# A sampling-and-scan loop: factors from three row groups, three selection banks, long matmuls set apart, GpSimd's sums in a row

## The chip, the cores and the metric

The kernel runs on one core of one Trainium2 chip. The metric is device time in microseconds (us) of one execution; the kernel before took 2436.45 us (median of three runs, 2435.26 to 2442.39).

## The reference, cut to what matters

Four convolutional blocks follow each other on a batch of 4 images of 64 channels and 128x128 pixels. Only the third block's second half matters here. Its input has been through a depthwise convolution; offsets were computed from it, and then:

```
out = tap(y0,x0,(1-wy)(1-wx)) + tap(y0,x0+1,(1-wy)wx) + tap(y0+1,x0,wy(1-wx)) + tap(y0+1,x0+1,wy*wx)   # bilinear sampling
x_dbl = x_proj_w @ out            # 8 rows for dt, 1 row B, 1 row C
delta = softplus(dt_w @ x_dbl[:8] + dt_b);   dA = exp(delta * A);   dBx = delta * B * out
h[t] = dA[t] * h[t-1] + dBx[t];   y[t] = C[t] * h[t] + Ds * out[t]    # along all pixels
x = x + out_proj( layernorm(y) )
```

## The kernel before, in words

Two images stand on the 128 partitions at once (2 x 64 channels), so the whole program runs twice ("pairs"). In the sampling loop an image pair is cut into 32 tiles of 4 rows, 128 x 512 elements. The offsets are small, so sampling is done with nine shifts: each pixel's nine factors are computed in a compact form (`W9`), split into three bf16 parts, transposed by a DMA into `WTB`, spread over the channels by TensorE, multiplied with the shifted image on VectorE, and the nine products are summed (four on TensorE into the bank `ACC`, five on GpSimd).

The loop is a software pipeline written out by hand. Each engine runs `step` for c = -2 to 35; `on(d)` says whether tile c+d exists, and the order of the statements in `step` is the order in the engine's queue, which is strict. T is the tile of step c. Semaphores count steps, `after(t)` is the count once tile t is done. All names below are used in the text that follows:

- VectorE (`sample_and_scan_dve`): `product(q)`, q = 0 to 8 (L856) reads the factors that `spread(q)` put in a PSUM bank; `t` (L863) and `x` (L867) scale and add the block's output for tile T-4; `bx` (L875), `scan` (L881), `hc` (L892) and `y` (L897) are the recurrence for tile T-2; `delta` (L907) is the softplus' last sum for tile T-1. `y` waits for `proj` of tile T-3, since it overwrites `YY`.
- TensorE (`sample_and_scan_pe`): `spread(q)` (L1066, bf16) alternates between two PSUM banks and waits for product q-2; `add_up(m)` (L1074, f32) sums product m; `center` (L1082), `mean` (L1090) and `proj` (L1092) are the layernorm and output projection of tile T-3; `WZ`, `WB`, `WC` (L1105, L1111, L1115) make the factors z, B and C of tile T-1 directly from the sampled tile with three f32 matmuls. In front of `WZ` the queue waits for GpSimd's last sum of tile T-1, for `delta` and for `scan` of tile T-2 (`sc_h`).
- ScalarE (`sample_and_scan_act`): hat functions of the offsets (L1004, L1008), `hi`, `mid` copies (L1041, L1043), square, Ln and Exp of the layernorm (L999, L1020, L1022), softplus of z (L1025 to L1030), the copy of the sampled tile out of `ACC` (L1035), and dA (L1048).
- GpSimd (`sample_and_scan_pool`): the factors (L955, L964, L970), the five sums `add(m)` (L948) and `UU` = delta times the sampled tile (L977).
- SyncE issues the DMA transposes, and at the kernel's start the loads of constants and the save `rt_spill`, whose landing (`rt_saved`) ScalarE and GpSimd wait for.

The lines that decide the order on TensorE around the three factor matmuls are, before:

```
                spread(5)
                if on(-1):
                    pe.wait_ge(df_add, summed(T - 1, POOL_SUMS - 1, POOL_SUMS))
                    pe.wait_ge(sc_delta, after(T - 2))
                    pe.wait_ge(sc_h, after(T - 2))
                    pe.matmul(PSUM[:, ZB, :], WZ[:, :], XS[:, (k + 1) % 2, :], ...).then_inc(sc_z, 1)
                spread(6)
```

Of the kernel before, what the change touches and what calls it, by code (L numbers as in the profile page):

```python
# [30 lines left out]
DT_RANK = 8  # L31
PW = W + 2
# [85 lines left out]
def program(nc, x, vec, mat, dts, rows, fc, sel, far_sel, cst, out):  # L118
    ctx = ExitStack()
    with ctx:  # L120
# [3 lines left out]
        def sem(name):  # L124
# [11 lines left out]
        WQ, WK, WV, WPROJ, WIN, WZ, WB, WC = (sb(n, [P, P]) for n in  # L136
            ("WQ", "WK", "WV", "WPROJ", "WIN", "WZ", "WB", "WC"))
# [30 lines left out]
        DTS = REG[0:DT_RANK, NMAT + 62 * P:NMAT + 62 * P + 3 * C]  # L168
# [110 lines left out]
        assert NMAT + 62 * P + 3 * C <= NREG - TOK - NRT  # L279
# [34 lines left out]
        ACC, ZB, BB, CB, MB, OB2 = 2, 3, 4, 5, 6, 7  # L314
# [15 lines left out]
        def steps(*ns):  # L330
# [37 lines left out]
        (sc_z, sc_bc, sc_abs, sc_exp, sc_ln, sc_delta, sc_u, sc_da, sc_bx, sc_h, sc_hc, sc_y, sc_cen, sc_proj, sc_sq, sc_var,  # L368
         sc_lv, sc_rs, sc_t, sc_x) = (sem(n) for n in (
            "sc_z", "sc_bc", "sc_abs", "sc_exp", "sc_ln", "sc_delta", "sc_u", "sc_da", "sc_bx", "sc_h", "sc_hc",  # L370
            "sc_y", "sc_cen", "sc_proj", "sc_sq", "sc_var", "sc_lv", "sc_rs", "sc_t", "sc_x"))
# [70 lines left out]

        def strip_done(pair, c):

            return pair * NS + (c + 1)
# [40 lines left out]
        def _(sp):  # L486
# [4 lines left out]
            sp.dma_start(DTS[:, :], dts).then_inc(load, 16)  # L491
# [12 lines left out]
            sp.wait_ge(const_act, 3)  # L504
            sp.dma_start(rt_spill, RT).then_inc(rt_saved, 16)
# [3 lines left out]
            with sp.Fori(0, PAIRS) as pair:  # L509
# [76 lines left out]
                sp.wait_ge(sc_delta, pair * NT + (NT + CREDIT))  # L586
# [244 lines left out]
        def sample_and_scan_dve(dve, pair, stats):  # L831
# [3 lines left out]
            def step(pair, c, b, on, far=False):  # L835
                T, k = pair * NT + c, b % 2

                def product(q):
                    if not on(0):
                        return  # L840
                    dy, dx = TAPS[q]
                    dve.wait_ge(df_w, turn(T, q))

                    if q == 0:
                        dve.wait_ge(df_acc, summed(T - 1, 3, PE_SUMS))
                    elif q == 1 and on(-1):
# [12 lines left out]
                product(0)
                if on(-4):  # L860
                    dve.wait_ge(sc_rs, after(T - 4))
                    dve.wait_ge(sc_proj, after(T - 4))
                    dve.tensor_tensor(PSUM[:, OB2, :], PSUM[:, OB2, :], RS2, ALU.mult).then_inc(sc_t, 1)  # L863
                product(1)
                if on(-4):
                    dve.wait_ge(sc_t, after(T - 4))
                    dve.scalar_tensor_tensor(out=xch(c - 4), in0=img(PSUM[:, OB2, :]), scalar=OUTB[:, :], in1=xch(c - 4),  # L867
                                             op0=ALU.add, op1=ALU.add,
                                             accum_out=sum_at[:, bass.ds(c - 4, 1)]).then_inc(sc_x, 1)
# [13 lines left out]
                if far and on(-1):  # L883

                    if on(0):
                        dve.wait_ge(df_acc, summed(T, PE_SUMS - 1, PE_SUMS))
                    dve.wait_ge(df_add, summed(T - 1, POOL_SUMS - 1, POOL_SUMS))
                    far_dve(dve, c - 1, (k + 1) % 2, reach)
                product(4)
# [12 lines left out]
                if on(-1):  # L902

                    dve.wait_ge(sc_ln, after(T - 1))
                    dve.wait_ge(sc_u, after(T - 2))
                    dve.wait_ge(sc_da, after(T - 2))
                    dve.tensor_tensor(RL, PSUM[:, ZB, :], AB, ALU.add).then_inc(sc_delta, 1)  # L907
# [14 lines left out]
        def sample_and_scan_pool(pool, pair):  # L922
# [9 lines left out]
            def step(pair, c, b, on, far=False):  # L932
# [26 lines left out]
                add(0)  # L959
# [5 lines left out]
                add(1)  # L965
                if on(2):
# [11 lines left out]
                add(3)  # L978
# [3 lines left out]
        def sample_and_scan_act(act, pair):  # L982
# [7 lines left out]
            def step(pair, c, b, on, far=False):  # L990
# [5 lines left out]
                if on(-3):  # L996
                    act.wait_ge(sc_cen, after(T - 3))
                    act.wait_ge(sc_t, after(T - 4))
                    act.activation(RS2, PSUM[:, MB, :], ACT.Square).then_inc(sc_sq, 1)  # L999
                if on(2):  # L1000
# [7 lines left out]
                    act.activation(HT, HT, ACT.Relu, bias=1.0, scale=-1.0).then_inc(df_hat, 1)  # L1008
                if on(-4):
# [7 lines left out]
                if on(-3):  # L1017

                    act.wait_ge(sc_var, after(T - 3))
                    act.activation(RS2, PSUM[:, MB, :], ACT.Ln, bias=GNE[:, 1:2]).then_inc(sc_lv, 1)  # L1020
                    act.wait_ge(sc_lv, after(T - 3))
                    act.activation(RS2, RS2, ACT.Exp, scale=-0.5).then_inc(sc_rs, 1)  # L1022
                if on(-1):
                    act.wait_ge(sc_z, after(T - 1))
                    act.activation(AB, PSUM[:, ZB, :], ACT.Abs, bias=vc("dt_b")).then_inc(sc_abs, 1)  # L1025
                    act.wait_ge(sc_abs, after(T - 1))
                    act.activation(PSUM[:, ZB, :], PSUM[:, ZB, :], ACT.Relu, bias=vc("dt_b"))
                    act.activation(AB, AB, ACT.Exp, scale=-1.0).then_inc(sc_exp, 1)
                    act.wait_ge(sc_exp, after(T - 1))
                    act.activation(AB, AB, ACT.Ln, bias=1.0).then_inc(sc_ln, 1)  # L1030
# [5 lines left out]
                if on(2):  # L1036
# [5 lines left out]
                    act.wait_ge(df_r1, after(T + 2))  # L1042
                    act.activation(part(1), top(REST), ACT.Copy).then_inc(df_mid, 1)  # L1043
                if on(-1):

                    act.wait_ge(sc_delta, after(T - 1))
                    act.wait_ge(sc_h, after(T - 2))
                    act.activation(DA, RL, ACT.Exp, scale=SM[:, 9:10]).then_inc(sc_da, 1)  # L1048
# [3 lines left out]
        def sample_and_scan_pe(pe, pair):  # L1052
# [3 lines left out]
            def step(pair, c, b, on, far=False):  # L1056
                T, k = pair * NT + c, b % 2

                def spread(q):

                    if on(0):
# [3 lines left out]
                        pe.wait_ge(df_p, turn(T, q - 2))  # L1065
                        pe.matmul(img(PSUM[:, (k + q) % 2, :]), SELB[:, q, :], WTB[0:WROWS, k, :, h, :],  # L1066
# [12 lines left out]
                if on(-3):  # L1079
                    pe.wait_ge(sc_y, after(T - 3))  # L1080
                    pe.wait_ge(sc_lv, after(T - 4))
                    pe.matmul(PSUM[:, MB, :], cs("center"), YY, start=True, stop=True).then_inc(sc_cen, 1)  # L1082
# [3 lines left out]
                add_up(1)  # L1086
                spread(4)
                if on(-3):
                    pe.wait_ge(sc_sq, after(T - 3))
                    pe.matmul(PSUM[:, MB, :], cs("mean"), RS2, start=True, stop=True).then_inc(sc_var, 1)  # L1090
                    pe.wait_ge(sc_x, after(T - 4))
                    pe.matmul(PSUM[:, OB2, :], WOUT2[:, :], YY, start=True, stop=True).then_inc(sc_proj, 1)  # L1092
                add_up(2)
                spread(5)
                if far:
                    add_up(3)
                if on(-1):
# [7 lines left out]
                    pe.matmul(PSUM[:, ZB, :], WZ[:, :], XS[:, (k + 1) % 2, :], start=True, stop=True).then_inc(sc_z, 1)  # L1105
                spread(6)
                if not far:
                    add_up(3)
                spread(7)
                if on(-1):  # L1110
                    pe.matmul(PSUM[:, BB, :], WB[:, :], XS[:, (k + 1) % 2, :], start=True, stop=True)  # L1111
                spread(8)
                if on(-1):
                    pe.wait_ge(sc_y, after(T - 2))
                    pe.matmul(PSUM[:, CB, :], WC[:, :], XS[:, (k + 1) % 2, :], start=True, stop=True).then_inc(sc_bc, 1)  # L1115
# [53 lines left out]
        def _(dve):  # L1169
# [4 lines left out]
            dve.wait_ge(load, 16 * 9)  # L1174

            for w in (WQ, WK, WV, WPROJ, WIN, WOUT, WZ, WB, WC):
                dve.memset(w[:, :], 0.0)
# [27 lines left out]
            for s in range(2):  # L1205
# [5 lines left out]
                xp = MAT["x_proj"][0]  # L1211
                for w, col in ((WB, DT_RANK), (WC, DT_RANK + 1)):
                    dve.tensor_copy(w[p:q, p:q], MATS[p:q, xp + col:xp + col + 1].broadcast_to([C, C]))
# [37 lines left out]
            for s in range(2):  # L1251
                p, q = s * C, s * C + C
                dve.tensor_copy(WZ[p:q, p:q], PSUM[p:q, 0, 0:C])
# [1231 lines left out]
```

## Time and profile before

| | |
|---|---|
| median of three runs | 2436.45 us |
| the profiled execution's own time | 2439.82 us |
| its span in the trace | 2438.0 us |
| busy share of the span: PE, DVE, ACT, POOL | 88%, 75%, 58%, 58% |
| granted TensorE clock, mean over the span | 0.929 |
| the two sampling loops | about 743 to 1110 us and 1938 to 2305 us |

In the trace PE is TensorE's matmul and PEld its weight load, DVE is VectorE, ACT ScalarE, POOL GpSimd and SP SyncE; L856 is line 856 of the kernel before. The span is what the trace covers; the execution's own time is 1.8 us longer. A record's duration overlaps the next one's on the same engine (VectorE's 128x512 operations last some 0.68 us and start 0.60 us apart), so distances between starts are what a queue costs. An f32 matmul of 512 columns shows as two records.

### The profile page before, as it was taken

What the parts mean: (1) busy time and instruction counts of PE and PEld (TensorE: products, weight loads), DVE (VectorE), ACT (ScalarE), POOL (GpSimd) and SP (SyncE); (2) the same over time, 40 slices, a digit from 0 to 9 for tenths busy, and PEclk for the clock granted to TensorE, in tenths of its full rate; (3) what the DMA queues carried; (4) which work ended last, traced back from release to release, by engine and by line L of the source; (5) the groups of instructions that cost most, each with busy time, mean ns of one, the idle gap of its engine ahead of it and who ended that gap; (6) DMA issues with size and microseconds to landing.
All of it is one profiled execution on the core that took longest, in us unless ns stands there. A gap on an engine that the chain in (4) does not pass through costs nothing. (4 is left out here: it accounts for less than half of the span.)

```text
span 2438.0 us, 28756 instructions
## 1 busy us (share of the span) xinstructions
PE 2135.2 (88%) x7363; PEld 1102.2 (45%) x7363; DVE 1834.2 (75%) x3128; ACT 1416.5 (58%) x2192; POOL 1417.2 (58%) x1305
## 2 busy tenths in 40 slices
PE   2998759798998999997988978698989799999798
PEld 2397435443553444433335954353435434444243
DVE  6555667499986999995755658566999589999754
ACT  1843444286884777763346437235868667777532
POOL 2233009398967989972322410484989499999532
PEclk9978879899998999998998979799989799999899
DMA  5000283500001212224820006534000022223244
GB/s 189 1 1 0 92 302 94 199 1 1 1 1 28 44 39 61 40 52 141 251 45 0 1 1 233 189 107 158 0 1 1 12 27 53 48 44 61 83 122 113
DMA packets 199339, 172.78 MB, mean 71 GB/s; under 512 B 72535, under 2 KB 175327, under 8 KB 195831
## 3 DMA queue, kind: packets, MB, share of 16 engines
q1 hardware_dynamic: 199159, 170.78, 24.8%
q8 instruction: 64, 1.05, 0.2%
q14 instruction: 116, 0.95, 0.1%
HBM read 81.69 MB, written 72.29 MB: 63 GB/s over the span
## 5 line engine op out<-in xcount | busy, mean ns | idle before, releaser
L948 POOL TENSOR_TENSOR BIG<-BIG 128x512 f32<-128x512 f32 x320 | 407.1, 1272 | 88.4 <-DVE BIG L856 78.4
L856 DVE TENSOR_TENSOR BIG<-PSUM,BIG 128x512 f32<-128x512 f32 x576 | 391.0, 682 | 59.0 <-PE PSUM L1066 30.7
L1138 DVE SCALAR_TENSOR_TENSOR PSUM<-BIG,VECS,PSUM 128x1024 f32<-128x1024 f32 x224 | 288.2, 1287 | 44.6 <-PE PSUM L2111 39.5
L1074 PE MATMUL PSUM<-BIG,CSTS 128*128 128x512 f32 x512 | 266.8, 602 | 0.0
L782 POOL TENSOR_TENSOR BIG<-TOEP,BIG 128x384 f32<-128x384 f32 x84 | 98.2, 1196 | 270.5 <-DVEq L1543 270.5
L2111 PE MATMUL PSUM<-BIG,WDW 128*128 128x512 f32 x512 | 236.4, 607 | 11.1 <-ACT BIG L2011 11.1
L1066 PE MATMUL PSUM<-BIG,SELB 120*128 120x512 bf16 x576 | 212.0, 386 | 16.7 <-issue 6.8
L2307 PE MATMUL PSUM<-BIG 128*128 128x381 f32 (+1 forms) x576 | 189.5, 493 | 12.9 <-DVE BIG L789 12.9
L1066 PEld LDWEIGHTS PSUM<-BIG,SELB 120*128 120x128 bf16 x576 | 55.3, 96 | 264.4 <-DVE BIG L856 190.9
L2111 PEld LDWEIGHTS PSUM<-BIG,WDW 128*128 128x128 f32 x512 | 99.3, 195 | 141.1 <-issue 122.4
L1784 POOL TENSOR_TENSOR BIG<-BIG 128x1024 f32<-128x1024 f32 x64 | 151.1, 2360 | 10.3 <-POOL BIG L1787 10.3
L2307 PEld LDWEIGHTS PSUM<-BIG 128*128 128x128 f32 x576 | 111.4, 194 | 90.5 <-ACT BIG L1962 13.5
L741 PE MATMUL PSUM<-BIG,WL 128*128 128x512 f32 x256 | 120.9, 617 | 15.2 <-POOL BIG L726 12.3
L725 POOL TENSOR_TENSOR BIG<-BIG 128x576 f32<-128x576 f32 x32 | 38.8, 1214 | 152.9 <-issue 92.6
L1074 PEld LDWEIGHTS PSUM<-BIG,CSTS 128*128 128x128 f32 x512 | 98.2, 195 | 58.6 <-issue 54.2
L1787 POOL TENSOR_SCALAR BIG<-BIG,VECS,CSTS 128x1024 f32<-128x1024 f32 x96 | 114.3, 1197 | 17.1 <-DVE PSUM L1593 11.2
L741 PE MATMUL PSUM<-BIG,WMID 128*128 128x512 f32 x256 | 115.3, 593 | 0.2 <-DVE BIG L716 0.2
L1972 ACT ACTIVATE BIG<-PSUM,SMG 128x1152 f32<-128x1152 f32 x32 | 39.1, 1221 | 121.7 <-PE PSUM L2307 108.4
L1793 POOL TENSOR_TENSOR BIG<-BIG 128x1024 f32<-128x1024 f32 x32 | 75.6, 2362 | 55.5 <-ACT BIG L1999 55.1
L1025 ACT ACTIVATE BIG<-PSUM,VECS 128x512 f32<-128x512 f32 x64 | 44.0, 687 | 108.4 <-PE PSUM L1105 108.4
L1999 ACT ACTIVATE BIG<-BIG,VECS 128x1024 f32<-128x1024 f32 x96 | 102.9, 1139 | 0.0
L1549 DVE SCALAR_TENSOR_TENSOR BIG<-BIG,SMG 128x1152 f32<-128x1152 f32 x32 | 54.2, 1693 | 54.6 <-ACT BIG L1972 54.6
(363 smaller groups left out, 5079.6 us busy)
## 6 DMA issues: line engine op xcount, KB each, us to landing
spill<-X SPq DMA_DIRECT2D x18, 1024.0 KB, 6.1
back_spill<-BIG SPq DMA_DIRECT2D x32, 576.0 KB, 3.4
X<-x SPq DMA_DIRECT2D x32, 512.0 KB, 7.5
rows_spill<-X SPq DMA_DIRECT2D x64, 256.0 KB, 4.1
out<-BIG SPq DMA_DIRECT2D x64, 256.0 KB, 3.6
BIG<-rows_spill SPq DMA_DIRECT2D x28, 512.0 KB, 5.3
X<-back_spill SPq DMA_DIRECT2D x14, 896.0 KB, 12.8
BIG<-fc SPq DMA_DIRECT2D x8, 1024.0 KB, 10.0
```

Source lines behind the costliest of these rows:

```text
L741: ins = pe.matmul(PSUM[:, 4 * k + m, :].rearrange("p (r j) -> p r j", r=8), w, VC[:, k, m, b:b + 8, :], start=(b == 0), stop=(b == 1))
L782: eng.tensor_tensor(to.rearrange("p (x c r) -> p x c r", x=3, r=WROW), TOEP[:, y].unsqueeze(1).unsqueeze(1).broadcast_to([P, 3, WCH, WROW] ...
L856: dve.tensor_tensor(img(product_buffer(b, q)), img(PSUM[:, (k + q) % 2, :]), pch(c, XBASE, dy, dx), ALU.mult).then_inc(df_p, 1)
L948: pool.tensor_tensor(a, a, x, ALU.add).then_inc(df_add, 1)
L1066: pe.matmul(img(PSUM[:, (k + q) % 2, :]), SELB[:, q, :], WTB[0:WROWS, k, :, h, :], start=True, stop=True).then_inc(df_w, 1)
L1074: pe.matmul(PSUM[:, ACC, :], ident, product_buffer(b, m), start=(m == 0), stop=(m == PE_SUMS - 1)).then_inc(df_acc, 1)
L1138: return dve.scalar_tensor_tensor(out=rows8(to), in0=strip(c, base, dy, dx), scalar=vc(weights, j), in1=rows8(acc), op0=ALU.mult, op1=ALU.add)
L1784: pool.tensor_tensor(d_side[:, c % 2, :], d_side[:, c % 2, :], d_tap, ALU.add).then_inc(d1_part, 1)
L1787: pool.tensor_scalar(rows8(d_tap if n else d_side[:, c % 2, :]), strip(c, XBASE, dy, dx), vc("dw_w", DW2_SIDE[n]), cs("zero")[:, 0:1], ALU ...
L1999: act.activation(rows8(a_side[:, j, c % 2, :]), strip(c, BASE, dy, dx), ACT.Identity, scale=vc("conv2d_w", j)).then_inc(d1_side, 1)
L2111: ins = pe.matmul(img(acc[:, h * CH:(h + 1) * CH]), w[:, j - stored, :], strip(c, base, dy, dx)[:, h * ROWS:(h + 1) * ROWS, :], start=(j = ...
L2307: ins = pe.matmul(to, WIDE[:, u % RING, x, :], v, start=(x == 1), stop=(x == 2))
```

## The change

On TensorE the three factor matmuls are replaced by two stages: `WX` (one f32 matmul of the sampled tile onto 96 rows: three groups of 32 rows, each with the ten rows of `x_proj` for both images), a copy of these 96 rows by ScalarE into `AB`, and then three f32 matmuls with 32 contracted rows each (`WG`), one per group, that write z, B and C into their banks. `spread` rotates over three banks (0, 1, 7) and waits for product q-3; `proj` writes the bank `MB`, which `center` and `mean` use too, so it now waits for Ln (`sc_lv`). The f32 matmuls are set apart by spreads. VectorE's `delta` moves from the end of step T-1's tile to the middle of the next step, `bx`, `scan` and `hc` follow each other behind product 4. GpSimd does its split first and then `add(0)` to `add(3)` without other work between. On ScalarE the `mid` copy and dA move to the next step's beginning, and the copy for `WX` is added. The buffers of the products are assigned differently. At the start the load of `dts` and the product that made `WZ` go, and six small loads of `WG` are issued ahead of `rt_spill`.

```diff
-        ACC, ZB, BB, CB, MB, OB2 = 2, 3, 4, 5, 6, 7
+        ACC, ZB, BB, CB, MB = 2, 3, 4, 5, 6
+        SPREADS = (0, 1, 7)
...
             sp.wait_ge(const_act, 3)
+            for s in range(2):
+                at, cols = s * XR, slice(s * C, (s + 1) * C)
+                sp.dma_start(WG[at:at + DT_RANK, cols], dts[:, 2 * C:3 * C]).then_inc(load, 16)
+                for r in (1, 2):
+                    row = r * 32 + at + DT_RANK + r - 1
+                    sp.dma_start(WG[row:row + 1, cols], cst[0:1, CST["one"][0]:CST["one"][0] + C]).then_inc(load, 16)
             sp.dma_start(rt_spill, RT).then_inc(rt_saved, 16)
...
# VectorE, step
                product(1)
                if on(-4):
...
+                if on(-2):
+                    dve.wait_ge(sc_ln, after(T - 2))
+                    dve.wait_ge(sc_u, after(T - 3))
+                    dve.wait_ge(sc_da, after(T - 3))
+                    dve.tensor_tensor(RL, PSUM[:, ZB, :], AB, ALU.add).then_inc(sc_delta, 1)
                 product(2)
+                product(3)
+                if not far:
+                    product(4)
                 if on(-2):
                     dve.wait_ge(sc_u, after(T - 2))
-                    dve.wait_ge(sc_bc, after(T - 2))
+                    dve.wait_ge(sc_zbc, all_three(T - 2))
                     dve.tensor_tensor(PSUM[:, BB, :], UU, PSUM[:, BB, :], ALU.mult).then_inc(sc_bx, 1)
-                product(3)
-                if on(-2):
                     dve.wait_ge(sc_bx, after(T - 2))
...
-                product(4)
                 if on(-2):
                     dve.wait_ge(sc_h, after(T - 2))
                     dve.tensor_tensor(PSUM[:, CB, :], HH[:, k, :], PSUM[:, CB, :], ALU.mult).then_inc(sc_hc, 1)
...
                 product(8)
-                if on(-1):
-                    dve.wait_ge(sc_ln, after(T - 1))
...
# GpSimd, step (after the three multiplies of W9)
-                add(0)
...
-                add(1)
...
+                add(0)
+                add(1)
                 add(2)
+                add(3)
                 if on(-1):
                     pool.wait_ge(sc_delta, after(T - 1))
...
-                add(3)
                 add(4)
# ScalarE, step
+                if on(-1):
+                    act.wait_ge(sc_xd, after(T - 1))
+                    act.wait_ge(sc_delta, after(T - 2))
+                    act.activation(AB[0:3 * 32, :], PSUM[0:3 * 32, ZB, :], ACT.Copy).then_inc(sc_copied, 1)
# TensorE, step
-                        pe.wait_ge(df_p, turn(T, q - 2))
-                        pe.matmul(img(PSUM[:, (k + q) % 2, :]), SELB[:, q, :], WTB[0:WROWS, k, :, h, :],
+                        if q >= 3 or on(-1):
+                            pe.wait_ge(df_p, turn(T, q - 3))
+                        pe.matmul(img(PSUM[:, SPREADS[q % 3], :]), SELB[:, q, :], WTB[0:WROWS, k, :, h, :],
                                   start=True, stop=True).then_inc(df_w, 1)
```

TensorE's order in one step is then, with its waits (those between `spread(6)` and `WX` are the old ones in front of `WZ`, unchanged):

```
spread 0, 1, 2; add_up 0; spread 3; add_up 1; center; spread 4; add_up 2; spread 5; mean; spread 6;
[wait df_add(T-1), sc_delta(T-2), sc_h(T-2)] WX; spread 7; [wait sc_lv(T-3)] proj; add_up 3; spread 8;
[wait sc_copied(T-1), sc_y(T-2)] three row-group matmuls
```

VectorE's is: product 0, t, product 1, x, delta, products 2, 3, 4, bx, scan, hc, product 5, [wait sc_proj(T-3)] y, products 6, 7, 8.

## Rows read from the trace of the kernel before

**Rows 1.** Windows: stretch, length, then busy us of PE, PEld, DVE, ACT, POOL; clock; DMA.
```profile
900.00:1000.00 100.00, 99.82 (x269) 41.11 (x268) 96.12 (x158) 74.04 (x156) 90.22 (x101) 1.00 0.22 45
```
**Rows 2.** Timeline of VectorE, one step: start us, duration us, line, operation, [idle before].
```profile
904.18 0.68 DVE L856 TENSOR_TENSOR BIG<-PSUM,BIG 128x512 f32<-128x512 f32 x1
...
905.98 0.74 DVE L867 SCALAR_TENSOR_TENSOR X<-PSUM,OUTB,X 128x512 f32<-128x512 f32 x1
...
906.64 0.69 DVE L856 TENSOR_TENSOR BIG<-PSUM,BIG 128x512 f32<-128x512 f32 x1
...
908.44 1.27 DVE L881 TENSOR_TENSOR_SCAN BIG<-BIG,PSUM 128x512 f32<-128x512 f32 x1
...
913.84 0.69 DVE L856 TENSOR_TENSOR BIG<-PSUM,BIG 128x512 f32<-128x512 f32 x1 [0.21 <-PE PSUM L1066]
...
917.51 0.68 DVE L856 TENSOR_TENSOR BIG<-PSUM,BIG 128x512 f32<-128x512 f32 x1
...
919.31 1.27 DVE L881 TENSOR_TENSOR_SCAN BIG<-BIG,PSUM 128x512 f32<-128x512 f32 x1
```
**Rows 3.** Timeline of TensorE, the same step.
```profile
907.39 0.39 PE L1066 MATMUL PSUM<-BIG,SELB 120*128 120x512 bf16 x1
907.61 1.02 PE L1090 MATMUL PSUM<-BIG,CSTS 128*128 128x512 f32 x2
908.48 1.02 PE L1092 MATMUL PSUM<-BIG,WOUT 128*128 128x512 f32 x2
...
913.43 0.38 PE L1066 MATMUL PSUM<-BIG,SELB 120*128 120x512 bf16 x1
```
**Rows 4.** Timeline of VectorE: the stage's first scan, then its end.
```profile
767.62 1.27 DVE L881 TENSOR_TENSOR_SCAN BIG<-BIG,SM,PSUM 128x512 f32<-128x512 f32 x1
...
1082.30 1.27 DVE L881 TENSOR_TENSOR_SCAN BIG<-BIG,PSUM 128x512 f32<-128x512 f32 x1
...
1090.81 0.70 DVE L875 TENSOR_TENSOR PSUM<-BIG,PSUM 128x512 f32<-128x512 f32 x1 [0.41 <-POOL BIG L977]
1091.54 1.28 DVE L881 TENSOR_TENSOR_SCAN BIG<-BIG,PSUM 128x512 f32<-128x512 f32 x1
1092.85 0.70 DVE L892 TENSOR_TENSOR PSUM<-BIG,PSUM 128x512 f32<-128x512 f32 x1
...
1097.23 0.69 DVE L907 TENSOR_TENSOR BIG<-PSUM,BIG 128x512 f32<-128x512 f32 x1 [2.90 <-ACT BIG L1030]
...
1109.88 0.75 DVE L867 SCALAR_TENSOR_TENSOR X<-PSUM,OUTB,X 128x512 f32<-128x512 f32 x1
```
**Rows 5.** Timeline at the stage's end: a TensorE matmul behind a wait, then ScalarE.
```profile
1093.45 1.12 PE L1105 MATMUL PSUM<-BIG,WZ 128*128 128x512 f32 x2 [1.13 <-POOL BIG L948]
1094.42 1.02 PE L1111 MATMUL PSUM<-BIG,WB 128*128 128x512 f32 x2
1094.62 0.69 ACT L1025 ACTIVATE BIG<-PSUM,VECS 128x512 f32<-128x512 f32 x1 [1.76 <-PE PSUM L1105]
```
**Rows 6.** Timeline of TensorE in the attention: row-group matmuls between full ones.
```profile
1441.07 1.13 PE L2197 MATMUL PSUM<-BIG 32*128 32x256 f32 x8
1442.14 1.09 PE L2210 MATMUL PSUM<-CSTS,BIG 128*128 128x128 f32 x8
1443.16 1.13 PE L2197 MATMUL PSUM<-BIG 32*128 32x256 f32 x8
```
**Rows 7.** Timeline at the kernel's start: SyncE's issues, and ScalarE that waits for them.
```profile
49.77 0.33 SPq L505 DMA_DIRECT2D rt_spill<-BIG  x1
50.14 0.48 SPq L507 DMA_DIRECT2D rows_spill<-CSTS  x1
...
52.69 0.60 SPq L508 DMA_DIRECT2D rows_spill<-CSTS  x1
...
54.81 1.28 ACT L1858 ACT_TABLE_LOAD   x1 [5.07 <-DMA rows_spill<-CSTS]
56.63 0.26 ACT L1852 ACTIVATE SM<-PSUM,GNE 128x1 f32<-128x1 f32 x1 [0.54 <-PE PSUM L2105]
```

More of the change, by code:

```diff
@@ L882, in step @@
                                            ALU.mult, ALU.add).then_inc(sc_h, 1)
[L883 to L888, printed above, removed]
-                product(4)
+                if far:
+                    if on(-1):
+                        if on(0):
+                            dve.wait_ge(df_acc, summed(T, PE_SUMS - 1, PE_SUMS))
+                        dve.wait_ge(df_add, summed(T - 1, POOL_SUMS - 1, POOL_SUMS))
+                        far_dve(dve, c - 1, (k + 1) % 2, reach)
+                    product(4)
                 if on(-2):
@@ L995, in step @@
                     act.preload_act_table_set("natural_log_exp_and_others")
[L996 to L999, printed above, removed]
+                if on(1):
+                    act.wait_ge(df_r1, after(T + 1))
+                    act.activation(part(1), top(REST), ACT.Copy).then_inc(df_mid, 1)
                 if on(2):
@@ L1016, in step @@
                                    bias=SHIFT, accum_out=sq_at[:, c - 4:c - 3]).then_inc(stats_done, 1)
[L1017 to L1022, printed above, removed]
-                if on(-1):
[L1024 to L1030, printed above, removed]
+                if on(-1):
+                    act.wait_ge(sc_xd, after(T - 1))
+                    act.wait_ge(sc_delta, after(T - 2))
+                    act.activation(AB[0:3 * 32, :], PSUM[0:3 * 32, ZB, :], ACT.Copy).then_inc(sc_copied, 1)
                 if on(0):
@@ L1078, in step @@
                 spread(1)
[L1079 to L1082, printed above, removed]
                 spread(2)
@@ L1086, in step @@
                 add_up(1)
+                if on(-3):
+                    pe.wait_ge(sc_y, after(T - 3))
+                    pe.wait_ge(sc_x, after(T - 4))
+                    pe.matmul(PSUM[:, MB, :], cs("center"), YY, start=True, stop=True).then_inc(sc_cen, 1)
                 spread(4)
+                add_up(2)
+                spread(5)
                 if on(-3):
@@ L1090, in step @@
                     pe.matmul(PSUM[:, MB, :], cs("mean"), RS2, start=True, stop=True).then_inc(sc_var, 1)
[L1091 to L1094, printed above, removed]
+                spread(6)
                 if far:
@@ L1104, in step @@
                         far_pe(pe, c - 1, reach)
[L1105 to L1106 removed]
+                    pe.matmul(PSUM[:, ZB, :], WX[:, :], XS[:, (k + 1) % 2, :], start=True, stop=True).then_inc(sc_xd, 1)
+                spread(7)
+                if on(-3):
+                    pe.wait_ge(sc_lv, after(T - 3))
+                    pe.matmul(PSUM[:, MB, :], WOUT2[:, :], YY, start=True, stop=True).then_inc(sc_proj, 1)
                 if not far:
                     add_up(3)
[L1109 to L1111 removed]
                 spread(8)
                 if on(-1):
+                    pe.wait_ge(sc_copied, copied(T - 1, 0))
                     pe.wait_ge(sc_y, after(T - 2))
[L1115 removed]
+                    settle(pe)
+                    for r, bank in enumerate((ZB, BB, CB)):
+                        rows = slice(r * 32, r * 32 + 32)
+                        pe.matmul(PSUM[:, bank, :], WG[rows, :], AB[rows, :], start=True, stop=True).then_inc(sc_zbc, 1)
             settle(pe)
@@ L1173, in _ @@
             dve.reg_mov(far_dve_turn, 0)
[L1174 to L1176 removed]
+            dve.wait_ge(load, 16 * 8)
+            for w in (WQ, WK, WV, WPROJ, WIN, WOUT, WX, WG):
                 dve.memset(w[:, :], 0.0)
```

92 lines of the change are left out of this document (48 added, 44 removed).

## The prediction

> **What bounds the kernel now.** The windows come first: in the steady sampling loop PE is busy 99.8 of 100 us, DVE 96.1, POOL 90.2 and ACT 74.0, at the full TensorE clock, 2.4 GHz [rows 1]. So three engines stand close together, and shares do not tell which one sets the step. The timeline does: scans follow each other by 10.87 us (908.44 to 919.31 [rows 2]), and one circle of waits adds up to just that. Product 8 starts at 913.84, product 2 of the next step 3.67 us later, behind VectorE's own work; 0.75 us after a product 2 (906.64) comes spread 4 (907.39), which waits for it because there are two banks; from there TensorE runs to spread 8 without a gap, 6.04 us (907.39 to 913.43), and 0.41 us later product 8 starts [rows 2, 3]. 3.67 + 0.75 + 6.04 + 0.41 = 10.87. The reader should see that the step is neither VectorE's nor TensorE's sum, but a chain that changes engines twice.
>
> **Prices.** VectorE's tensor-tensor operations start 0.60 us apart (904.18 to 905.98 holds three), the scalar-tensor-tensor ones 0.66 (905.98 to 906.64) [rows 2]. One that waits for the operation directly in front of it costs more: bx to scan 0.73, scan to hc 1.31 [rows 4]. A spread takes 0.22, an f32 matmul 0.87, its record 1.02 [rows 3]; behind a wait an f32 matmul takes 0.97 to the next one [rows 5]. A reader of PSUM starts 0.03 to 0.05 us after the record's end (913.43 + 0.38 to 913.84; 1093.45 + 1.12 to 1094.62) [rows 2, 3, 5]; I take 0.05 for TensorE behind VectorE too.
>
> **Part 1, the banks and the long matmuls.** With three banks spread q waits for product q-3, and the circle above is gone. What is left on VectorE is the sum of its queue: nine products 5.40, t, delta and hc 1.80, x and y 1.32, bx 0.73, scan 1.31, together 10.56 us; bx, scan and hc now stand in a row and pay 0.25 of it. TensorE's sum is nine spreads 1.98, eight f32 matmuls 6.96 (four add_ups, center, mean, proj, WX), the three row groups and the change to them and back.
>
> **Part 2, the row groups.** The loop before has none; the attention has. There eight records of 32 contracted rows and 256 columns and eight full ones of 128 columns take 2.09 us together (1441.07 to 1443.16) [rows 6]. From 0.87 for two passes of 512 columns, a pass of 256 is 0.217 and one of 128 is 0.109. One after another the first eight alone would take 1.74 and all 2.61; in pairs they take 0.87, with the eight full ones 1.74, and 0.35 is left for going over and back. So row groups do run side by side, and I price the three at 0.87 + 0.35. The lower bound is 0.87; the upper, one after another, 2.61 + 0.35. TensorE's sum: 1.98 + 6.96 + 1.22 = 10.16 us.
>
> The Trainium skill (TensorE: Matmul & The Clock Gate, Part 3: Packing small matmuls) gives four row groups of 512 columns a speed-up of 3.07 instead of 4. By that page three groups would take an estimated 4 x 0.87 / 3.07 = 1.13 instead of 0.87, and the time would come out some 14 us above mine; rows 6 show full overlap, but of two groups only.
>
> **Part 3, what takes the old circle's place.** The wait in front of WX is the one that stood in front of WZ: scan of tile T-2 must be done. Before, scan came behind product 3 and TensorE met the wait late. Now scan stands behind delta and product 4, and spread 7, proj, add_up 3, spread 8 and the row groups are all queued behind WX. VectorE's y waits for proj, because YY is overwritten. That closes a circle:
> - scan to y: scan 1.27, start 0.05, WX 0.97, spread 7 0.22, proj 1.02, start 0.03: 3.56 us (VectorE alone would reach y after 1.31 + 0.60 + 0.60 = 2.51).
> - y to the next scan, VectorE's queue without a gap: y 0.66, products 6 to 8 1.80, product 0, t, product 1 1.80, x 0.66, delta 0.60, products 2 to 4 1.80, bx 0.73: 8.05 us.
>
> Together 11.61. A second circle goes through spread 0 of the next step, which stands behind the row groups: scan 1.27, 0.05, WX 0.97, spread 7 0.22, proj 0.87, add_up 0.87, spread 8 0.22, row groups 0.87, over and back 0.35, spread 0 to product 0 0.39 + 0.03: 6.11; product 0 to scan 1.80 + 0.66 + 0.60 + 1.80 + 0.73 = 5.59: 11.70. A third goes through the softplus: to the row groups' end 5.75, Abs to delta 2.61 (1094.62 to 1097.23 [rows 4, 5]), delta to scan 3.13: 11.49. The longest sets the step: **11.70 us, 0.83 more than before**. Is TensorE at WX by the time scan ends? In that order it has passed spread 6 about 0.4 us after scan starts, so yes: it then idles about 0.9 us.
>
> The Trainium skill (VectorE: DVE Perf Modes, The DRAIN you can't avoid) says that a semaphore between chained operations costs nothing extra. By that page bx to scan would be 0.60, each circle 0.13 shorter, and the time an estimated 7 us below mine; rows 4 show 0.73, so the trace disagrees.
>
> **What is hidden.** ScalarE gets one more copy, at most the 0.69 of an Abs [rows 5]: 7.4 + 0.7 = 8.1 us a step, with room; the copy itself lies beside spread 7, proj, add_up and spread 8 (2.18 us), and longer than that it would delay the row groups one for one. GpSimd's 9.0 us a step [rows 1] are only reordered; its UU waits for the later delta, and bx for UU: from delta's start 0.7 + 1.3 against 2.4 us of products, so 0.4 is spare. The mid copy and with it the DMA transpose move to the next step's start; spread 0 that reads the result comes some 8 us after, and if that cover went, product 0 would wait. The six small loads are needed only hundreds of us later.
>
> **Sum.** Between the first scan and the one at 1082.30 lie 29 steps, 314.68 us, 10.85 each [rows 4]. After: 27 at 11.70, and two at some 11.0, in which t, x and proj are still missing: 337.9, so +23.2 us. The fill before the first scan has the third bank and no scan to wait for: -1 (-2.5 to +1). The end, from 1082.30 to the last x at 1109.88, is a chain of single operations [rows 4]: the last tile's factors now need a copy and the groups (0.7 + 0.35 + 0.87 = +1.9), WX waits for the scan before it (+1.2), and proj for Ln (about +1): +4 (1 to 7). That is 26.2 for a pair, 52.4 for two. At the start SyncE issues six small loads ahead of rt_spill, at 0.37 (49.77 to 50.14) to 0.73 us each (49.77 to 52.69 holds four): 2.2 to 4.4; ScalarE's table load waits for the end of these issues and has 0.54 spare [rows 7]; VectorE's and SyncE's shorter preparation gives up to 1 back: +2 (0 to 4). In all +54. The sum is made on the profiled execution, whose own 2439.82 us (span 2438.0) are 3.4 above the median; I put the difference on the median, 2436.45: **2490 us**.
>
> **Rivals.**
> - *Faster:* WX's wait is already met when TensorE comes to it (as it would be if it asked for the scan of a tile earlier), and VectorE's sum is the step: 10.56, or -0.31 for 54 steps, -17, and +8 from the fill, the ends and the start: 2428 us. It decides if TensorE passes spread 6 later than scan ends, 0.9 us from my reckoning, and even then scan to y stays a chain. For it: the third bank removes today's circle. Against: the order in the code.
> - *The groups do not run side by side*, so that factors by groups save nothing: circle two gets 1.74 longer, 13.4 a step, 54 times: 2584 us. Against: rows 6.
> - *The clock falls.* PE idles about 1.5 of 11.7 us; if it were granted 1.2 GHz, circle one's WX, spread and proj would double, +2.2 a step: 2609 us; half the time, 2550. For it: idle gaps that rows 1 do not have; against: they are short.
>
> **How the numbers follow.** My forecast gets 0.80, the faster rival 0.10, the groups 0.05, the clock 0.05. The forecast's own bounds: circles of 11.4 to 12.0 us (54 times -0.3 to +0.3, 16 us), the fill, ends and start -12 to +13 (their ranges above, added up but for a third): 2462 to 2519; I let the upper end reach to 2525, towards a clock that falls in some steps. That leaves out the rivals, 2 in 10. A measurement tells 0.3%, 7 us, from no change. The faster rival lies just beyond that bound, so it is split: faster 0.07, same 0.03, slower 0.90.
>
> **What would show it.** Scans 11.7 us apart; PE idle in front of WX, released by scan; y with an idle time released by proj, or product 0 by spread 0; the three groups within a few hundredths of a us of each other, followed by the next spread after about 1.1; PE busy near 87%. Wrong if scans are under 10.9 us apart, if VectorE shows no idle at y and at product 0, or if the clock in the loop is below 1.0.

## The result, and the profile after

The changed kernel takes 2510.56 us (median of four runs, 2507.08 to 2513.3); the kernel before 2439.15 (four runs, the three from ahead of the prediction among them). The ratio is 1.0293, 95% interval 1.0269 to 1.0316: 71 us slower, where +54 and 2490 us were forecast. The profiled execution's span is 2511.5 us, against 2438.0 before, +73.5.

The windows of the changed kernel, over the same stretch and with the same columns as [rows 1]:

```profile
900.00:1000.00 100.00, 91.39 (x265) 32.87 (x263) 89.05 (x143) 73.25 (x151) 84.65 (x96) 1.00 0.21 43
```

Every engine is less busy than before, and the clock is still at its full level, 2.4 GHz. So no engine's sum sets the step; something is waited for. The page's costliest groups name it (busy us, mean ns; idle us before, and what ended most of it):

```profile
L1122 PE MATMUL PSUM<-BIG,WX 128*128 128x512 f32 x128 | 73.1, 653 | 49.8 <-DVE BIG L897 48.2
```

L897 is the scan, L1122 is WX: TensorE stands 48 us in front of WX until a scan is done, 0.75 for each of 64 tiles. Two timelines show what that does. VectorE, one step (start, duration, line, operation, [idle before, what ended it]), to be read beside [rows 2]; L897 is scan, L914 y, L865 the products, L893 bx:

```profile
911.98 1.28 DVE L897 TENSOR_TENSOR_SCAN BIG<-BIG,PSUM 128x512 f32<-128x512 f32 x1
...
915.69 0.75 DVE L914 SCALAR_TENSOR_TENSOR BIG<-BIG,VECS,PSUM 128x512 f32<-128x512 f32 x1 [1.11 <-PE PSUM L1126]
916.35 2.48 DVE L865 TENSOR_TENSOR BIG<-PSUM,BIG 128x512 f32<-128x512 f32 x4
...
923.01 0.69 DVE L893 TENSOR_TENSOR PSUM<-BIG,PSUM 128x512 f32<-128x512 f32 x1
923.73 1.28 DVE L897 TENSOR_TENSOR_SCAN BIG<-BIG,PSUM 128x512 f32<-128x512 f32 x1
```

TensorE, the same step; L1084 is spread, L1126 proj, L1137 the row groups:

```profile
912.31 0.38 PE L1084 MATMUL PSUM<-BIG,SELB 120*128 120x512 bf16 x1
913.41 1.10 PE L1122 MATMUL PSUM<-BIG,WX 128*128 128x512 f32 x2 [0.71 <-DVE BIG L897]
914.34 0.38 PE L1084 MATMUL PSUM<-BIG,SELB 120*128 120x512 bf16 x1
914.56 1.02 PE L1126 MATMUL PSUM<-BIG,WOUT 128*128 128x512 f32 x2
...
916.28 0.38 PE L1084 MATMUL PSUM<-BIG,SELB 120*128 120x512 bf16 x1
916.59 1.13 PE L1137 MATMUL PSUM<-BIG,WG 32*128 32x512 f32 x6
917.65 1.03 PE L1084 MATMUL PSUM<-BIG,SELB 120*128 120x512 bf16 x3
```

Scans are 11.75 us apart. The circle reads off the two fences: scan 911.98, WX 913.41, proj 914.56, y 915.69 after 1.11 us of idle, and from y VectorE works without a gap to the next scan, 8.04 us. 3.71 + 8.04 = 11.75. Product 0 of the next step, the last of the four products at 916.35, has no gap in front of it, so the circle through spread 0 is not the one that binds: spread 0's record ends at 918.03 (917.65 + 0.38), product 0 starts at 918.15 (the fourth of the four, 3 x 0.60 behind 916.35), some 0.1 us later than it had to.

**Where the 73.5 us lie.** On VectorE, first scan, last scan of the steady steps, the y that waits, and the last t and x of the first pair, to be read beside [rows 4]:

```profile
769.02 1.28 DVE L897 TENSOR_TENSOR_SCAN BIG<-BIG,SM,PSUM 128x512 f32<-128x512 f32 x1
...
1112.05 1.28 DVE L897 TENSOR_TENSOR_SCAN BIG<-BIG,PSUM 128x512 f32<-128x512 f32 x1
...
1128.52 0.75 DVE L914 SCALAR_TENSOR_TENSOR BIG<-BIG,VECS,PSUM 128x512 f32<-128x512 f32 x1 [3.18 <-PE PSUM L1126]
...
1148.12 0.70 DVE L872 TENSOR_TENSOR PSUM<-PSUM,BIG 128x512 f32<-128x512 f32 x1 [7.92 <-PE PSUM L1126]
1148.86 0.75 DVE L876 SCALAR_TENSOR_TENSOR X<-PSUM,OUTB,X 128x512 f32<-128x512 f32 x1
```

| stretch | before | after | difference | forecast |
|---|---|---|---|---|
| pair 1: start to the first product 0 | 743.96 | 745.37 | +1.4 | +2 |
| first product 0 to first scan | 23.66 | 23.65 | 0.0 | -1 |
| 29 steady steps | 314.68 | 343.03 | +28.4 | +23.2 |
| the end, from the last steady scan to the last x | 27.58 | 36.81 | +9.2 | +4 |
| between the pairs' loops | 828.74 | 829.86 | +1.1 | 0 |
| pair 2: the same three stretches | 365.90 | 399.24 | +33.3 | +26.2 |
| the rest | 133.48 | 133.54 | +0.1 | 0 |

Pair 2's are -0.6, +25.0 (339.64 against 314.65) and +8.9 (36.51 against 27.58). The steps carry 53 us of the loss, where 46 were forecast; the two ends carry 18, where 8 were.

TensorE at the end of the first pair (L1104 is center, L1110 mean) shows why:

```profile
1119.85 1.10 PE L1104 MATMUL PSUM<-BIG,CSTS 128*128 128x512 f32 x2 [2.06 <-DVE X L876]
1121.63 2.07 PE L1110 MATMUL PSUM<-BIG,CSTS 128*128 128x512 f32 x2 [0.69 <-ACT BIG L1022]
1124.75 2.05 PE L1122 MATMUL PSUM<-BIG,WX 128*128 128x512 f32 x2 [1.05 <-DVE BIG L897]
...
1140.36 2.05 PE L1104 MATMUL PSUM<-BIG,CSTS 128*128 128x512 f32 x2 [2.67 <-DVE X L876]
1143.09 2.08 PE L1110 MATMUL PSUM<-BIG,CSTS 128*128 128x512 f32 x2 [0.69 <-ACT BIG L1022]
1145.94 2.08 PE L1126 MATMUL PSUM<-BIG,WOUT 128*128 128x512 f32 x2 [0.78 <-ACT BIG L1031]
```

Two things are to be seen. An f32 matmul that takes 1.02 to 1.13 us elsewhere takes 2.05 to 2.08 here: the clock is at its lower level, 1.2 GHz, again and again. And center waits for VectorE's x of the tile before, proj for ScalarE's Ln, because center, mean, proj, t and x all use the bank MB and take turns. The same fall of the clock stands at the loop's beginning, where TensorE idles 2.36 us until the first scan is done:

```profile
770.45 2.04 PE L1122 MATMUL PSUM<-BIG,WX 128*128 128x512 f32 x2 [2.36 <-DVE BIG L897]
...
772.71 1.92 PE L1092 MATMUL PSUM<-BIG,CSTS 128*128 128x512 f32 x2
```

The first interval between scans is 13.74 us there. In pair 2 TensorE idles the same 2.36 us at that place, the clock does not fall, and the interval is 10.74.

### The profile page after: what moved, and what is told of

Same layout as the page of the kernel before. It is cut to its first block and busy times, and to the rows that moved or that the text cites. A ratio compares the mean times of both kernels' runs of the same rounds, so it can differ in the third digit from the quotient of the medians.

```text
span 2511.5 us, 29190 instructions
## 1 busy us (share of the span) xinstructions
PE 2135.8 (85%) x7489; PEld 1065.2 (42%) x7489; DVE 1838.0 (73%) x3123; ACT 1458.3 (58%) x2256; POOL 1425.8 (57%) x1305
## 5 line engine op out<-in xcount | busy, mean ns | idle before, releaser
L865 DVE TENSOR_TENSOR BIG<-PSUM,BIG 128x512 f32<-128x512 f32 x576 | 367.2, 683 | 33.9 <-PE PSUM L1084 24.9
L1092 PE MATMUL PSUM<-BIG,CSTS 128*128 128x512 f32 x512 | 277.8, 624 | 15.2 <-DVE BIG L865 15.0
L796 POOL TENSOR_TENSOR BIG<-TOEP,BIG 128x384 f32<-128x384 f32 x84 | 83.6, 1023 | 272.4 <-DVEq L1561 272.4
L1084 PE MATMUL PSUM<-BIG,SELB 120*128 120x512 bf16 x576 | 209.8, 386 | 12.0 <-DMA BIG<-BIG 7.8
L1092 PEld LDWEIGHTS PSUM<-BIG,CSTS 128*128 128x128 f32 x512 | 87.0, 190 | 126.7 <-DVE BIG L865 95.5
L1084 PEld LDWEIGHTS PSUM<-BIG,SELB 120*128 120x128 bf16 x576 | 52.4, 97 | 185.6 <-issue 126.5
L1122 PE MATMUL PSUM<-BIG,WX 128*128 128x512 f32 x128 | 73.1, 653 | 49.8 <-DVE BIG L897 48.2
L1051 ACT ACTIVATE BIG<-PSUM 128x512 f32<-128x512 f32 x64 | 38.3, 598 | 107.8 <-PE PSUM L1092 106.0
```

The source lines that it names most:

```text
L865: dve.tensor_tensor(img(product_buffer(b, q)), img(PSUM[:, SPREADS[q % 3], :]), pch(c, XBASE, dy, dx), ALU.mult).then_inc(df_p, 1)
L1084: pe.matmul(img(PSUM[:, SPREADS[q % 3], :]), SELB[:, q, :], WTB[0:WROWS, k, :, h, :], start=True, stop=True).then_inc(df_w, 1)
L1092: pe.matmul(PSUM[:, ACC, :], ident, product_buffer(b, m), start=(m == 0), stop=(m == PE_SUMS - 1)).then_inc(df_acc, 1)
L1122: pe.matmul(PSUM[:, ZB, :], WX[:, :], XS[:, (k + 1) % 2, :], start=True, stop=True).then_inc(sc_xd, 1)
```

## The experiments

Theory: the wait for scan in front of WX closes a circle, scan, WX, proj, y, scan, and that circle is the step. Rivals: another circle of the same length stands right behind it (through spread 0, or the softplus), so that the wait alone is worth little; or VectorE's new order (bx, scan and hc in a row) costs the time. The first four runs share one set of times of the kernel before (median 2434.71 us), the last four another (2434.58).

**no_scan_wait.** WX no longer waits for scan; the waits for delta of tile T-2 (in front of WX) and for y of tile T-2 (in front of the row groups) stay, and these cover the banks that are overwritten. (The branch `far`, for larger offsets, keeps the wait.)

```diff
                     pe.wait_ge(df_add, summed(T - 1, POOL_SUMS - 1, POOL_SUMS))
                     pe.wait_ge(sc_delta, after(T - 2))
-                    pe.wait_ge(sc_h, after(T - 2))
```

> The changed kernel without the wait for scan in front of WX (its results are still safe: the row groups, which overwrite the banks that scan reads, wait for y, and y follows scan). Theory: the circle scan - WX - spread 7 - proj - y - next scan sets the step. Then WX starts when spread 6 is through, 0.55 us behind scan's start instead of 1.43, proj starts behind it at about 1.6 (Ln is done at 1.2), y comes 2.7 behind scan instead of 3.7 and the step falls from 11.75 to 10.7 to 10.9 us: about 2450 to 2460 us. Rival 1: y waits for proj because proj now shares its bank and waits for Ln; then WX moves but y does not: 11.7 a step, about 2510. Rival 2: the row groups' own circle (through spread 0 and the softplus) is as long as it was reckoned with the scan wait: 11.4 to 11.6 a step, about 2490 to 2500.

Measured: 2448.04 us, ratio 1.0060 (1.0038 to 1.0081). TensorE, then VectorE:

```profile
957.67 1.02 PE L1122 MATMUL PSUM<-BIG,WX 128*128 128x512 f32 x2
...
958.75 1.02 PE L1126 MATMUL PSUM<-BIG,WOUT 128*128 128x512 f32 x2
```
```profile
957.11 1.28 DVE L897 TENSOR_TENSOR_SCAN BIG<-BIG,PSUM 128x512 f32<-128x512 f32 x1
...
959.88 0.75 DVE L914 SCALAR_TENSOR_TENSOR BIG<-BIG,VECS,PSUM 128x512 f32<-128x512 f32 x1 [0.16 <-PE PSUM L1126]
960.54 2.48 DVE L865 TENSOR_TENSOR BIG<-PSUM,BIG 128x512 f32<-128x512 f32 x4
...
967.91 1.28 DVE L897 TENSOR_TENSOR_SCAN BIG<-BIG,PSUM 128x512 f32<-128x512 f32 x1
```

WX starts 0.56 us after scan starts, without idle; y's gap shrinks from 1.11 to 0.16 and the step is 10.80. This one wait, an old line that the change left alone, holds all the loss in the steps: without it they are 0.07 us shorter than before. Yet the kernel is still slower than the one before, because its ends (35.05 us from the last steady scan to the last x) are 7.5 us longer than [rows 4] shows, in each pair.

**proj_first.** The wait stays, proj is moved ahead of it. This was meant to open the circle through y and to leave the one through spread 0.

```diff
                 spread(6)
+                [wait sc_lv(T-3)] proj
                 [wait df_add(T-1), sc_delta(T-2), sc_h(T-2)] WX
                 spread(7)
-                [wait sc_lv(T-3)] proj
                 add_up(3)
```

> The changed kernel with the scan wait kept, but proj stands ahead of WX in TensorE's queue. Theory: two circles of nearly the same length; the one through y is opened (proj ends 2.4 behind scan's start, before y is due at 2.5), the one through WX, add_up, the row groups and spread 0 stays: product 0 about 6.0 behind scan, 11.6 a step, about 2500 us; VectorE's idle time moves from y to products 8 and 0. Rival: the stall at y is all there is; then it goes and the step is 10.7 to 10.8, about 2455.

Measured: 2490.94 us, ratio 1.0234 (1.0196 to 1.0272), step 11.57. VectorE's scan, y and, behind products 6 to 8, product 0; then TensorE's proj, WX, spreads 0 to 2 and add_up 0 (L1092):

```profile
950.77 1.28 DVE L897 TENSOR_TENSOR_SCAN BIG<-BIG,PSUM 128x512 f32<-128x512 f32 x1
...
953.29 0.74 DVE L914 SCALAR_TENSOR_TENSOR BIG<-BIG,VECS,PSUM 128x512 f32<-128x512 f32 x1
...
956.75 0.69 DVE L865 TENSOR_TENSOR BIG<-PSUM,BIG 128x512 f32<-128x512 f32 x1 [0.69 <-PE PSUM L1084]
```
```profile
952.04 1.12 PE L1114 MATMUL PSUM<-BIG,WOUT 128*128 128x512 f32 x2 [0.56 <-ACT BIG L1031]
953.01 1.02 PE L1125 MATMUL PSUM<-BIG,WX 128*128 128x512 f32 x2
...
956.32 0.82 PE L1084 MATMUL PSUM<-BIG,SELB 120*128 120x512 bf16 x3
957.49 1.12 PE L1092 MATMUL PSUM<-BIG,CSTS 128*128 128x512 f32 x2 [0.35 <-DVE BIG L865]
```

The idle time moved from y to product 0, released by a spread (L1084), and time and step came near what the theory expected. But the circle that binds here is another one. Scan is over at 952.05 and WX starts only at 953.01, straight behind proj: it is proj, now ahead of WX, that waits 0.56 us, for ScalarE's Ln (L1031). From product 0 the way goes to add_up 0 (0.74), over add_up 1, center and mean to Ln and proj (6.12, to 963.61), to WX (0.97), to the next spread 0 (3.31) and to product 0 (0.43), together 11.57, and scan is not on it. So the run put one wait in front of WX in the place of another; it does not show the circle through scan and spread 0. Moving proj gains 0.18 us a step, removing the wait for scan 0.95.

**products_between.** no_scan_wait with VectorE's order changed: products 5, 6 and 7 stand between bx, scan, hc and y, as products did in the kernel before.

```diff
-bx, scan, hc, product 5, y, products 6, 7, 8
+bx, product 5, scan, product 6, hc, product 7, y, product 8
```

> As no_scan_wait, and VectorE's order is product 4, bx, product 5, scan, product 6, hc, product 7, y, product 8, so that no operation waits for the one right in front of it. Rival (VectorE's queue is the bound once the scan wait is gone): its sum falls from 10.56 to 10.3 and the step by 0.2, 10 us below no_scan_wait. Theory of circles: y is now some 1.8 us later behind scan, and the row groups wait for y; from y's end over the groups (1.1) and spread 0 to product 0, and over the softplus to delta (3.9), the way is longer than VectorE's work beside it: 11.2 to 11.4 us a step, 2480 to 2490, slower than no_scan_wait though VectorE has less to do.

Measured: 2480.69 us, ratio 1.0182 (1.0141 to 1.0223), step 11.36. VectorE's y and product 0, then TensorE's row groups (L1140 here):

```profile
955.68 0.74 DVE L919 SCALAR_TENSOR_TENSOR BIG<-BIG,VECS,PSUM 128x512 f32<-128x512 f32 x1
...
958.02 0.69 DVE L865 TENSOR_TENSOR BIG<-PSUM,BIG 128x512 f32<-128x512 f32 x1 [1.00 <-PE PSUM L1087]
```
```profile
956.52 1.13 PE L1140 MATMUL PSUM<-BIG,WG 32*128 32x512 f32 x6 [0.55 <-issue]
957.59 0.82 PE L1087 MATMUL PSUM<-BIG,SELB 120*128 120x512 bf16 x3
```

VectorE's self-waits are gone, 0.25 us of its sum by the prediction's prices, and yet the step is 0.56 longer than in no_scan_wait: the row groups wait for y (955.68 + 0.74, groups at 956.52), and a late y makes spread 0 and product 0 late. So, without the wait for scan, the order in a row is the better one; it is not what costs the time.

**two_banks.** no_scan_wait with two selection banks, as before.

```diff
-if q >= 3 or on(-1):  pe.wait_ge(df_p, turn(T, q - 3));  bank SPREADS[q % 3]
+if q >= 2 or on(-1):  pe.wait_ge(df_p, turn(T, q - 2));  bank (k + q) % 2
```

> As no_scan_wait, but the spreads alternate between two banks and wait for product q-2 as in the kernel before. Theory: with VectorE's new order (bx, scan and hc in front of product 5) spread 7 must wait for product 5, which ends 2.6 behind scan's start, and proj and y stand behind it: y 3.9 behind scan, 12.0 a step, about 2520 us, so the third bank is worth over 1 us a step in this order. Rival: the third bank is worth only what the old circle had over VectorE's sum: 10.9 to 11.0 a step, 2460 to 2470.

Measured: 2573.21 us, ratio 1.0564 (1.0524 to 1.0605), step 12.88, some of 14.45. TensorE:

```profile
956.20 0.39 PE L1084 MATMUL PSUM<-BIG,SELB 120*128 120x512 bf16 x1 [1.01 <-DVE BIG L865]
956.42 1.02 PE L1126 MATMUL PSUM<-BIG,WOUT 128*128 128x512 f32 x2
...
958.96 0.39 PE L1084 MATMUL PSUM<-BIG,SELB 120*128 120x512 bf16 x1 [0.66 <-DVE BIG L865]
```

The direction was expected, the size not: spread 7 waits for product 5, proj stands behind it and y behind proj, so one late spread delays y by 1.42 us, and spread 8 then waits again. In this order the third bank is worth 2.1 us a step (12.88 against 10.80). The steps of 14.45, five in the first pair and none in the second, are steps in which the clock fell: 0.88 over one of them, 1.00 over the one behind it.

**proj_next.** What is left on VectorE in no_scan_wait is y's 0.16 us. Spread 7 goes behind proj.

```diff
                 WX
-                spread(7)
                 proj
+                spread(7)
                 add_up(3)
```

> no_scan_wait, with spread 7 behind proj instead of ahead of it. Theory (without the scan wait, y's 0.16 us behind proj is the only gap on VectorE, and its sum of 10.64 the next bound): y starts without idle, the step is 10.64 us, time 2438 to 2442. Rival (TensorE's own sum with the wait for product 0 in front of add_up 0 sets it): the step stays 10.75 to 10.80, time 2446 to 2450.

Measured: 2445.17 us, ratio 1.0042 (1.0025 to 1.0059), step 10.74. VectorE:

```profile
955.50 1.28 DVE L897 TENSOR_TENSOR_SCAN BIG<-BIG,PSUM 128x512 f32<-128x512 f32 x1
...
958.04 0.75 DVE L914 SCALAR_TENSOR_TENSOR BIG<-BIG,VECS,PSUM 128x512 f32<-128x512 f32 x1
958.71 2.64 DVE L865 TENSOR_TENSOR BIG<-PSUM,BIG 128x512 f32<-128x512 f32 x4
...
966.25 1.28 DVE L897 TENSOR_TENSOR_SCAN BIG<-BIG,PSUM 128x512 f32<-128x512 f32 x1
```

The theory was wrong: y's gap is gone, but four products now take 2.64 instead of 2.48. The last of them, product 0, starts 0.05 us behind the end of spread 0's record (960.23 + 0.38), and TensorE's add_up 0 waits for product 0 and then runs to the next spread 0 without a gap. That is the rival's mechanism, at 10.74 where it had 10.75 to 10.80: 0.06 below no_scan_wait and 0.16 above VectorE's own 10.58 (2.54 from scan to y here, 8.04 from y to scan without a gap, as in the changed kernel).

**end_banks.** The ends of no_scan_wait: where no spreads are left, proj writes one of their banks.

```diff
+in steps c >= 32: proj writes bank (0, 1)[c % 2], straight behind center, without the wait for sc_lv
+t and x of the next step read that bank; center of steps c >= 33 waits sc_lv(T-4) instead of sc_x(T-4)
```

> no_scan_wait, but in the last steps (no spreads left) proj writes a free spread bank instead of MB, straight behind center and without the wait for Ln; center then waits for Ln of the tile before instead of for x. Theory (the ends of the changed kernel are long because center, mean, proj, t and x share one bank and take turns in it, besides the clock): the step stays 10.8 us; from the last scan of the steady steps to the last x, 35.8 us in no_scan_wait and 27.6 in the kernel before, becomes 29 to 32; time 2436 to 2442 us. Rival (it is TensorE's clock in the ends alone): 35 or more, time 2446 to 2450.

Measured: 2439.98 us, ratio 1.0019 (1.0005 to 1.0033); from the last steady scan (1080.07) to the last x (1110.41) 30.34 us. (The 35.8 in the expectations for no_scan_wait runs to the end of x; from start to start, as everywhere else here, it is 35.05.) VectorE does not wait for proj any more, neither at y nor at the last t, whose releaser is now ScalarE. TensorE's clock is 0.89 over this end (1080 to 1111), against 0.71 in no_scan_wait, so a part of the 4.7 us gained can be the clock's; no run separates the two.

```profile
1092.44 0.75 DVE L923 SCALAR_TENSOR_TENSOR BIG<-BIG,VECS,PSUM 128x512 f32<-128x512 f32 x1
...
1109.68 0.70 DVE L881 TENSOR_TENSOR PSUM<-PSUM,BIG 128x512 f32<-128x512 f32 x1 [5.56 <-ACT BIG L1042]
1110.41 0.75 DVE L885 SCALAR_TENSOR_TENSOR X<-PSUM,OUTB,X 128x512 f32<-128x512 f32 x1
```

**end_clock.** no_scan_wait with f32 matmuls (`mean` by a constant tile) into the unused bank 7 in the last three steps, where TensorE waits; nothing reads them.

```diff
+step 32: 768 columns ahead of center;  step 34: 1024 ahead of center
+steps 32 to 34: 256 (step 33: 512) ahead of mean, 256 ahead of proj;  step 32: 256 ahead of the row groups
```

> no_scan_wait, with f32 matmuls into an unused bank in the last three steps, put where TensorE waits, so that it idles less there. Theory (half of the loss at the ends is 1.2 GHz): center, mean, WX and proj of the ends take 0.87 to 1.02 us again instead of 1.8 to 2.1, the stretch from the last steady scan to the last x becomes 30 to 33 us instead of 35.8, time 2438 to 2444. Rival (the waits, not the clock): the matmuls get short, yet the stretch stays above 34, time 2446 or more. If the clock stays at 1.2 GHz, the added matmuls make the stretch longer, 36 to 39.

Measured: 2441.51 us, ratio 1.0021 (1.0007 to 1.0036); 1074.72 to 1106.83, 32.11 us. The windows over the end, first of no_scan_wait, then of end_clock (the last three numbers are clock, DMA share and GB/s):

```profile
1076.00:1111.00 35.00, 23.16 (x42) 6.44 (x40) 18.09 (x28) 17.80 (x32) 8.87 (x8) 0.71 0.26 83
```
```profile
1075.00:1107.00 32.00, 24.72 (x64) 9.70 (x62) 18.02 (x28) 17.81 (x32) 8.85 (x7) 0.95 0.28 90
```

The work of the other engines is the same; TensorE is busy 1.56 us longer and the stretch is 3 us shorter. Work that computes nothing pays for itself by the clock here.

**three_edits.** proj_next, end_banks and end_clock together, on no_scan_wait. Since proj of the last steps stands straight behind center here, no columns stand ahead of it; step 34 has 1536 ahead of center instead of 1024.

> no_scan_wait with all three: proj next to WX, free banks and added matmuls in the ends. If they add up, the step is 10.64 us and the stretch from the last steady scan to the last x 26 to 30 us: 2448 - 9 - 2 x 7, 2420 to 2430 us, faster than the kernel before. If the ends give nothing, 2438 to 2442.

Measured: 2429.38 us, ratio 0.9978 (0.9962 to 0.9994): the only version faster than both kernels, by 5 us, 0.2%, against the one before (1.5 to 9 by the interval). The step is 10.74, as in proj_next, not 10.64. VectorE, last steady scan to last x, 28.14 us, and the window of that end:

```profile
1077.46 1.28 DVE L906 TENSOR_TENSOR_SCAN BIG<-BIG,PSUM 128x512 f32<-128x512 f32 x1
...
1105.60 0.75 DVE L885 SCALAR_TENSOR_TENSOR X<-PSUM,OUTB,X 128x512 f32<-128x512 f32 x1
```
```profile
1080.00:1106.00 26.00, 19.43 (x54) 7.60 (x52) 15.96 (x26) 15.84 (x29) 8.86 (x7) 1.00 0.25 91
```

So the 9.2 us that the change added to each end come apart: removing scan's wait takes 1.8 (36.81 to 35.05), and the banks, the clock and proj's place take 6.9 more (35.05 to 28.14); 0.6 stays. By themselves the banks took 4.7, the clock 2.9 and proj's place 1.8 (33.27 in proj_next), which is more than the three take together, so their gains overlap.

## Why the prediction was right, and which term was too small

**The circle** was right in its cause, the wait for scan in front of WX, and nearly in its length; which circle binds was not. It reckoned 11.61 through y, 11.70 through spread 0 and 11.49 through the softplus, and took the longest. The one through y binds, at 11.75: WX starts 0.15 us behind the end of scan's record instead of 0.05, and y 0.11 behind proj's instead of 0.03, less 0.04 on WX itself; y to scan was 8.05 and is 8.04. The two delays at WX lie on spread 0's circle too. That this circle fell behind comes from two terms of about the same size: the 0.08 at y's start, which is not on it, and the row groups, 1.37 us from spread 8 to the next spread (916.28 to 917.65), where 0.22 + 0.87 + 0.35 = 1.44 was taken. So it is in part luck that the 11.70 of the wrong circle comes so near to 11.75. no_scan_wait shows that the wait is the cause. That the second circle lies some 0.1 us below is read from the rows of the changed kernel alone; in no run does it bind.

**The row groups.** By the Trainium skill (TensorE: Matmul & The Clock Gate, Part 3: Packing small matmuls) three groups would have taken an estimated 1.13 and the switch on top. The trace does not bear that out: the 1.37, less 0.22 for spread 8, leaves 1.15 for all three groups and the way to them and back, 0.28 more than one plain f32 matmul of 0.87. No run separates the groups from the way.

**bx to scan.** The Trainium skill (VectorE: DVE Perf Modes, The DRAIN you can't avoid) has a semaphore between chained operations for free, as it measured on copies; here bx to scan is 0.72 (923.01 to 923.73) against 0.60 otherwise, so the trace still disagrees, and the forecast had been made with the longer one.

**The steps' sum** was +23.2 a pair and is +28.4 and +25.0. 27 steps at 11.75 instead of 11.70 make 1.4; the second of the two early intervals is as long as the others, 11.75 instead of 11.0, 0.8; in pair 1 the first is 13.74, because the clock fell, 2.7; one interval, 12.12, is 0.4 too long, as one is in the first pair of no_scan_wait, end_banks and end_clock too (11.17; no run looked for its cause).

**The end** is the term that was mis-sized: "+4 (1 to 7)" for each pair, measured +9.2 and +8.9, outside its bounds. The three delays that it named are there, but it left out that center now waits for x of the tile before (2.06 and 2.67 us of idle time in the rows of the end), and each f32 matmul on that chain was priced as in the steady loop. The end's chain in the changed kernel has longer gaps, and behind them the clock stood at 0.72 over 1112 to 1149, against 0.88 over 1082 to 1110 before. That the clock falls was in the prediction as a rival for the whole loop, 0.05; it did not fall there (1.00), and it did at the loop's two edges, which no case priced.

**The start** (+2 forecast, +1.4 in this pair of traces) is not settled: the first product 0 starts anywhere from 737.7 (proj_next) to 746.9 us (products_between) in the kernels run here, though all but the one before have the same code ahead of it.

**Smaller slips.** One sign was missed: PE is busy 91.4 of 100 us, not near 87. The view counts a record to its end and shows 0.91 us of idle time a step (0.71 in front of WX, 0.20 in front of add_up 0), where the forecast went by 1.5 between the queue's prices. The 7.4 us of ScalarE and 9.0 of GpSimd "a step" are what [rows 1] show for each 10 us; a step of 10.87 held 8.0 and 9.8. Neither engine set the step, so nothing hangs on it. The range's "-12 to +13" does not come out of its terms either: added up in full they give -11 to +12, less a third -7 to +8, and 2490 + 16 + 8 would still have held the measured time.

**The rivals.** "Faster" asked for WX's wait to be already met; no_scan_wait is that kernel, and its step is 10.80 rather than the 10.56 given, with the ends still in the way. Groups one after another, 2.61 us, are refuted by the 1.06 from the first group to the next spread.

## What to carry to other kernels

A wait that cost nothing where it stood (scan in front of a late matmul) can become the step when either side of it is reordered: follow what is queued behind the waiting instruction, up to the other engine's next wait, and add up the circle. The fill and the drain of a software pipeline want prices of their own, since waits there can also cost TensorE's clock, and the users of a bank that is shared without harm in the steady loop wait for each other there. When a change loses, look for the one line: here all of the loop's loss hung on one wait, and without it, with proj's place and the ends mended, the new order is 5 us faster than the old one.

## What the runs showed of the hardware that was not expected

- Three f32 matmuls of 32 rows by 512 columns on different row groups start 0.006 us apart in the trace, each in two passes 0.53 us apart, and cost 1.15 us with the change of shape there and back (1.37 from the spread ahead of them to the one behind, less that spread's 0.22).
- An f32 matmul that waits for a VectorE scan starts 0.15 us behind the end of its record; one that waits for nothing follows the one before it at 0.86.
- TensorE kept 2.4 GHz through gaps of 0.71 and 0.20 us in each step of 11.75, and was at 1.2 GHz behind one gap of 2.36 us at the first pair's loop start (behind the same gap in the second pair it was not), and in the ends behind gaps of 2.06 and 0.69 with one matmul of 1.10 between them. With matmuls put into such gaps the granted clock over the end was 0.95 (end_clock), with the free banks besides 1.00 (three_edits).
